# Making the first four tiles' queries in two halves, in a fused decoder layer on one core

## The reference, cut to what matters

```python
x = _layernorm(x + _L0_attn_ref(x, ...))      # S4D long convolution by FFT, then its own layernorm
x = _layernorm(x + _L0_xattn_ref(x, ctx, ctx, ...))   # 16 heads of 16 over 77 keys
x = _layernorm(x + _L0_ffn_ref(x, ...))       # gated MLP of 1024 plus product-key experts
# cross attention:
qh = (q @ Wq.T + bq).reshape(B, Nq, H, D).transpose(0, 2, 1, 3)
attn = jax.nn.softmax(jnp.einsum('bhqd,bhkd->bhqk', qh, kh) * scale, axis=-1)
return (attn @ vh).transpose(0, 2, 1, 3).reshape(B, Nq, C) @ Wo.T + bo
```

## Time and profile before

| | |
|---|---|
| median of three runs | 693.98 us (689.98 to 695.78) |
| the profiled execution's own time | 689.71 us |
| its span | 687.9 us |
| TensorE matmul busy | 599.0 us (87%), 3200 instructions |
| VectorE, ScalarE, GpSimd busy | 484.3, 403.9, 308.5 us |
| mean granted TensorE clock | 0.920 of full speed |

### The profile page before, as it was taken

One profiled execution on the slowest core, in us unless ns is written; L12 is line 12 of the kernel. 1 busy time (PEld: TensorE's weight loads), 2 busy tenths in 40 slices (PEclk: granted clock), 3 DMA queues, 4 the chain that ended last, 5 costly groups with the idle time before them and its releaser, 6 DMA issues.

```text
span 687.9 us, 9791 instructions
## 1 busy us (share of the span) xinstructions
PE 599.0 (87%) x3200; PEld 393.4 (57%) x3200; DVE 484.3 (70%) x955; ACT 403.9 (59%) x595; POOL 308.5 (45%) x354
## 2 busy tenths in 40 slices
PE   6809588795769598999999999999999999899896
PEld 2503477573636364454776745578565478453485
DVE  7976475662346885897857789765779796678782
ACT  3865446222143265996673878773778774677760
POOL 3704975554142456352263632243735243744441
PEclk9858879899695677999999999999999999999999
DMA  8994020368161000000000000000000000000000
GB/s 272 309 235 90 1 76 27 101 171 224 27 247 59 1 1 1 0 2 0 1 0 1 17 8 9 0 1 1 8 16 1 9 1 1 9 15 9 0 9 23
DMA packets 19613, 34.14 MB, mean 50 GB/s; under 512 B 7273, under 2 KB 13931, under 8 KB 18219
## 3 DMA queue, kind: packets, MB, share of 16 engines
q1 hardware_dynamic: 15179, 29.33, 14.8%
q10 hardware_dynamic: 4384, 4.20, 1.9%
HBM read 21.81 MB, written 10.65 MB: 47 GB/s over the span
## 4 chain that ended last, share of the span: by engine, by line
PE 64%; DVE 12%; DMA 6%; ACT 6%; POOL 6%; issue 5%; SPq 1%; DVEq 0%; POOLq 0%; ACTq 0%
PE banks L804 20%; PE banks L894 8%; PE banks L899 8%; PE banks L849 4%; PE banks L871 4%; PE banks L826 3%; DMA scr_x<-arena 3%; PE banks L861 3%; PE banks L679 2%; PE banks L746 2%; PE banks L835 2%; DMA scr_v<-arena 2%; PE banks L886 2%; DVE stats L1437 2%; PE banks L716 1%
## 5 line engine op out<-in xcount | busy, mean ns | idle before, releaser
L1260 POOL TENSOR_TENSOR arena<-arena 128x1024 f32<-128x1024 f32 x64 | 123.3, 1927 | 159.1 <-ACT arena L1122 158.3
L804 PE MATMUL banks<-arena 128*128 128x512 f32 x384 | 174.4, 596 | 5.3 <-issue 3.7
L804 PEld LDWEIGHTS banks<-arena 128*128 128x128 f32 x384 | 69.8, 190 | 83.0 <-issue 76.9
L1122 ACT ACTIVATE arena<-arena 128x1024 f32<-128x1024 f32 x64 | 73.5, 1149 | 7.5 <-DVE arena L1525 3.0
L1124 ACT ACTIVATE arena<-arena 128x1024 f32<-128x1024 f32 x64 | 73.5, 1149 | 2.1
L1525 DVE SCALAR_TENSOR_TENSOR arena<-arena 128x1024 f32<-128x1024 f32 x48 | 63.9, 1331 | 1.7
L1012 ACT COPY arena<-banks 128x512 f32<-128x512 f32 (+1 forms) x64 | 34.1, 532 | 46.2 <-PE banks L796 30.3
L894 PE MATMUL banks<-arena 128*128 128x256 f32 x256 | 58.4, 381 | 2.4 <-DVE arena L1547 2.2
L1233 POOL TENSOR_SCALAR arena<-mv 128x1 f32<-128x1 f32 (+1 forms) x40 | 14.4, 361 | 102.1 <-DVE mv L1438 100.7
L899 PE MATMUL banks<-arena 128*128 128x256 f32 x256 | 57.9, 379 | 0.0
L1026 ACT ACTIVATE tok<-tok,arena,rstd 128x256 f32<-128x256 f32 x48 | 27.9, 598 | 44.0 <-POOL arena L1238 43.0
(11 more groups left out here) (179 smaller groups left out, 1096.3 us busy)
## 6 DMA issues: line engine op xcount, KB each, us to landing
scr_x<-arena SPq DMA_DIRECT2D x16, 256.0 KB, 8.9
arena<-scr_x SPq DMA_DIRECT2D x4, 1024.0 KB, 11.0
scr_z<-arena ACTq DMA_DIRECT2D x14, 256.0 KB, 3.8
tok<-in_x SPq DMA_DIRECT2D x8, 256.0 KB, 6.1
arena<-scr_z SPq DMA_DIRECT2D x4, 512.0 KB
out<-tok SPq DMA_DIRECT2D x16, 128.0 KB, 1.7
arena<-scr_z SPq DMA_DIRECT2D x2, 640.0 KB
arena<-in_imat SPq DMA_DIRECT2D x1, 1152.0 KB, 5.5
```

The source lines that it names most:

```text
L804: ins = mm(bk[:, :], w[:, k, P * m:P * m + P], src[:, k, :], start=(k == 0), stop=(k == KC - 1))
L1122: fn(ebuf[m % 2], sxb[m % 2], ACT.Prelu, bias=negt[:, n % 2, h:h + 1], alpha=FAR).then_inc(s_ranked, 1)
L1260: tt(sxb[m % 2], sim[:, n % 2, h, 0:XR].unsqueeze(2).broadcast_to((P, XR, NKEYS)), sim[:, n % 2, FH + h, :].unsqueeze(1).broadcast_to((P, ...
```

## The change

The queries of group 0 are made in two halves of 256 tokens (two tiles) each. Half 0 needs only turn1(0,0), half 1 needs turn1(0,1). Each half is a matmul of 256 columns instead of 512, twice as often, and takes a PSUM bank of its own; ScalarE moves each half by itself. Scores of tiles 0 and 1 wait for half 0, those of tiles 2 and 3 for half 1. The other three groups are made as before.

```diff
+         "query_first": (-0.08, -0.07, 0.114, 0.2684), "score_first": (0.0, 0.108), "turn2": (-0.001, 0.0655),
-         "ln": (-1.672, -1.4036, 0.3158, 1.2242, 1.9402, 2.3725, 3.0344, 3.1428),
-         "ln_steps": (-0.409, -0.234, 0.162, 0.013, 0.361), "sines": (-2.943, -2.336), "tables": (0.152,),
+         "ln": (-1.721, -1.4035, 0.316, 1.2245, 2.021, 2.373, 3.035, 3.1435),
+         "ln_steps": (-0.347, -0.234, 0.162, 0.013, 0.361), "sines": (-2.943, -2.336), "tables": (0.152,),
...
-       ("dve", "ln"): -0.302, ("dve", "residual"): -0.025, ("pool", "turn1"): 0.518, ("pool", "turn2"): 0.089,
+       ("dve", "ln"): -0.518, ("dve", "residual"): -0.025, ("pool", "turn1"): 0.518, ("pool", "turn2"): 0.089,
...
     def queries(start, s):
         for kind in ("turn1", "query"):
             for j in range(2):
-                put(start, kind, s, j, j=j)
+                if kind == "query" and s == 0:
+                    for half in range(2):
+                        put(start, kind, s, j, half, key="query_first", j=2 * half + j)
+                else:
+                    put(start, kind, s, j, j=j)
...
     for h in range(2):
-        put(-1, "score", 0, h, j=h)
+        put(-1, "score", 0, h, key="score_first", j=h)
...
+        def query_of(tl, hh):
+            return ("query", 0, hh, tl // 2) if tl < SUPER else ("query", tl // SUPER, hh)
+        def query_cols(step):
+            return slice(W // 2 * step[3], W // 2 * (step[3] + 1)) if step[1] == 0 else slice(0, W)
...
-                    pe.wait_ge(s_tev, T_AT[("turn1", n, 1)] + 1)
-                    wide(step + ("a",), wq, step[2], x1T)
+                    pe.wait_ge(s_tev, T_AT[("turn1", n, step[3] if n == 0 else 1)] + 1)
+                    wide(step + ("a",), wq, step[2], x1T, query_cols(step))
...
-                    pe.wait_ge(s_wact, ACT_TURN[("query", n // SUPER, hh, "a")])
+                    pe.wait_ge(s_wact, ACT_TURN[query_of(n, hh) + ("a",)])
...
-                    fn(qT[:, j, :], src, ACT.Identity, bias=pcol[:, j:j + 1]).then_inc(s_wact, 1)
+                    fn(qT[:, j, query_cols(step)], src[:, query_cols(step)], ACT.Identity,
+                       bias=pcol[:, j:j + 1]).then_inc(s_wact, 1)
```

More of the change, by code:

```diff
@@ L55 @@
 PAIRS = [(0, NC)] + [(2 * m - 1, 2 * m) for m in range(1, FREQ - 1)] + [(NC - 1,)]
[L58 to L63, removed]
-         "ln": (-1.672, -1.4036, 0.3158, 1.2242, 1.9402, 2.3725, 3.0344, 3.1428),
-         "ln_steps": (-0.409, -0.234, 0.162, 0.013, 0.361), "sines": (-2.943, -2.336), "tables": (0.152,),
+PLACE = {"probs": (0.166, 0.2592, 0.441), "score": (0.273, 0.6341), "attend": (0.592,), "turno": (0.772,),
+         "project": (1.4,), "project_last": (0.934,), "turn1": (-0.087, 0.0432), "query": (0.245, 0.2685),
+         "query_first": (-0.08, -0.07, 0.114, 0.2684), "score_first": (0.0, 0.108), "turn2": (-0.001, 0.0655),
+         "sim": (0.379,), "sim_first": (0.031,), "best": (0.432,), "best_first": (0.207,),
+         "pair": (0.283, 0.3903, 0.7922, 0.8026), "total": (0.847,), "first": (-0.1,), "sums": (-0.805,),
+         "exps": (-0.131,), "late": (-0.027, 0.0082, 0.7012),
+         "conv": (-2.338, -1.7115, -1.497, -1.4195, -1.329, -1.2905, -1.172, -0.9595),
+         "ln": (-1.721, -1.4035, 0.316, 1.2245, 2.021, 2.373, 3.035, 3.1435),
+         "ln_steps": (-0.347, -0.234, 0.162, 0.013, 0.361), "sines": (-2.943, -2.336), "tables": (0.152,),
          "taps": (0.982,), "x_second": (-2.2, 0.237), "skip": (1.3, 0.3), "k_first": (5.915, 0.66, 9.6, 0.247),
@@ L69 @@
          "inverse": (9.103, 0.13, 10.25, 0.11), "products": (0.0, 1.0, 0.0, 0.996, 0.0, 0.802, -0.084, 0.975),
-         "probs_alone": (0.016, 0.079, 0.473), "score_alone": (0.367, 0.6874), "attend_alone": (0.566,),
+         "probs_alone": (0.016, 0.0791, 0.4732), "score_alone": (0.367, 0.6875), "attend_alone": (0.566,),
          "turno_alone": (0.734,), "project_alone": (0.979,), "dev2": (0.031,), "norm2": (0.093,), "dev3": (0.402,),
@@ L798, in turn_tokens, with wide @@
                 ins.then_inc(s_tmm, 1)
-            def wide(key, w, m, src):
+            def wide(key, w, m, src, cols_of=slice(0, W)):
                 bk = w_unit(key)
                 for k in range(KC):
-                    ins = mm(bk[:, :], w[:, k, P * m:P * m + P], src[:, k, :], start=(k == 0), stop=(k == KC - 1))
+                    ins = mm(bk[:, cols_of], w[:, k, P * m:P * m + P], src[:, k, cols_of], start=(k == 0), stop=(k == KC - 1))
                 ins.then_inc(s_wmm, 1)
@@ L1051, in _ @@
                     if n:
-                        act.wait_ge(*W_DONE[W_AT[("query", n - 1, KC - 1, "a")]])
+                        act.wait_ge(*W_DONE[W_AT[query_of(SUPER * n - 1, KC - 1) + ("a",)]])
                     turned_tokens(step, step[2], x1T)
```

## The result

The changed kernel takes 686.76 us (median of 11 runs, 684.66 to 689.97) against 692.68 us for the kernel before in 11 runs beside it. The ratio is 0.9923 (95% interval 0.9895 to 0.9950): 5.3 us faster, between 3.5 and 7.3. The forecast was 691.0 us and a gain of 3.0 us, with a range of 686.5 to 695.5. The time lies in the range, 0.26 us above its low end, and inside the 1% that I called no change. Of the 4.2 us between forecast and time, 1.3 come from the kernel before, whose median was 693.98 us in the three runs that the forecast starts from and 692.68 in the eleven here. The mechanism and its sign were right; one term was too small.

What follows compares the result with a forecast made beforehand. The ramp's serial first tiles, with no engine full, bounded what could change. 3.6 us won at the probabilities' transposes less 0.65 given back makes 2.95, say 3.0: 691.0 us against a median of 693.98, range 686.5 to 695.5.

Steps and rivals of the forecast that it cites:

- (a): GpSimd at the start: dev1 0 goes before dev0 1, takes 1.59 us instead of 2.24 and ends at 190.58.
- (b): ScalarE at the start: norm1 0 runs from 190.62 to 191.72 instead of from 191.32.
- (c): TensorE: half queries of 0.93 us end at 194.5 and 195.4, half reads take 0.48, score(0,0) runs to 196.25.
- (e): VectorE: score(0,0) from 196.3 to 197.95 and score(0,1) from 199.5 to 201.15, no ln between them.
- (f): ScalarE: exponentials wait behind second-half queries; probabilities' transposes start at 203.05 instead of 206.69, 3.6 us earlier.
- (d): Price of GpSimd's swap: residual 1 starts at 191.7 instead of 188.86; norm1 1 ends 2.75 us later.
- What is given back: At turno 1 on TensorE: ln 5 before attend 1 on VectorE makes it wait, losing 0.65 us of the gain.
- What is kept behind it: From tile 0's transposes to the end: 3.6 us carried to project 0, 2.95 to 3.0 to turn2(0,0) and the end.
- rival 2: Tile 0 and turno 2 to project 2: full clock holds, 3 us more gain, 688.0 us; chance 0.20.
- The carrying: From turno 1 on: 2.95 to 3.0 us of gain reaches turn2(0,0) and the end of the kernel.
- Rival 1: Ramp: clock falls before 198 us and is half from 249 to 257; 2.3 us slower, 696.3 us; chance 0.12.
- rival 3: Behind the start: an unseen wait takes the gain, nothing carried, 694 us; chance 0.18.

Runs made afterwards that it cites:

- e2: Changed kernel with the old numbers for ln, ln_steps and VectorE's ln offset, so halves without the new lists: ratio 0.9941 to the kernel before.
- e1: Kernel before with the new numbers for ln, ln_steps and VectorE's ln offset, queries whole: ratio 1.0073 to the kernel before, 5 us slower.
- e3: Changed kernel with ln 5 back behind attend 1 on VectorE: ratio 0.9934 to the kernel before.
- e4: Changed kernel with dev1 4 back ahead of dev2 1 on GpSimd: ratio 0.9958 to the kernel before, 2.9 us faster.
- e9: Kernel before with four half queries put where the two whole ones stood, old numbers for everything else: ratio 0.9959 to the kernel before.
- e10: Kernel before with ln 2 to ln 5 moved into VectorE's idle time, queries whole: ratio 0.9976 to the kernel before.
- e8: Changed kernel with 18 idle products on TensorE in its pause before conv 0: ratio 0.9932 to the kernel before.
- e11: Changed kernel with ln 2 to ln 5 moved into VectorE's waits: ratio 0.9835 to the kernel before; medians of all executions 684.17 against 691.17 us.
- e6: Kernel before with idle products filling TensorE's pauses in the ramp: ratio 0.9962 to the kernel before, 2.6 us faster.
- e7: Changed kernel with idle products filling TensorE's pauses in the ramp: ratio 0.9900 to the kernel before, from four executions.
- e12: Kernel of e11 with 24 idle products before conv 0 and more in the ramp: ratio 0.9820 to the kernel before; medians 680.71 against 690.65 us.

## Why the prediction was right

**The start.** 3.26 us at the transposes against 3.6. The times of steps (a), (b), (c) and (e), counted from residual 0, stand within 0.3 us. Residual 1 starts at 6.38 us (forecast 6.3) and norm1 1 at 11.63 (11.4). Step (f) named what decides: the exponential behind query(0,1,1). Its two half queries took 1.99 us and not 1.85.

**The price of GpSimd's swap, step (d).** It is there (2.94 us at residual 1) but costs nothing at the transposes: without it they come at 18.17 (e2). The sentence that the first half alone would have allowed more left out conv 7. With whole queries the same swap, with the rest of the new lists, costs 5 us (e1).

**What is given back.** 0.65 us at turno 1: 0.70 in the trace (5.36 less 4.66), 0.76 in e3. **What I cost at nothing**, dev2 1 before dev1 4: nothing (e4).

**The step that was too small.** "What is kept behind it" carried 3.6 us to project 0 and let TensorE keep the half clock of before, 8.0 us from the transposes on. It took 4.3 us (206.02 to 210.36), because the clock held; project 0 moved by 5.36 us. I had that as one half of rival 2, with 1.4 to 2 us and a chance of 0.20, and wrote that nothing in the rows fixes when the clock falls. The other half of rival 2, full clock at turno 2 and project 2, did not come: turno 2 took 0.69 us and project 2 1.97, both at half. And the reason that I gave for the first half was wrong: the clock did not fall at 207 us, the old time of day, but at 211.3, behind attend 0. It was not chance either: the clock had fallen by tile 0's transposes in both traces of before and in e1, e9 and e10, and held to the end of attend 0 in all six traces with score(0,0) moved forward and no idle products at tile 0 (after, e2, e3, e4, e8, e11). What I should have looked at is TensorE's pauses ahead of that step: 1.90 and 2.95 us with one score product of 0.79 us between them before (both traces), and 1.76 us now. With the pauses filled the clock stays full past project 1 in both kernels (e6, e7), so it is for want of work in the pauses that it falls. Their length alone does not fix when: with 1.90 and 2.60 us (e10) it fell and came back before attend 0, and in the changed kernel the products behind a pause of only 1.52 us, after attend 0, ran at half clock. So the rows of before name the place, but not whether the clock would hold there.

This term, 2.1 us, makes most of the difference: with it the gain is 4.66 us at project 1, where the forecast had 2.95. The timed 5.3 us (3.5 to 7.3) fits that and can't be told from 4.7. The Trainium skill, TensorE: Matmul & The Clock Gate, "HAM oscillation — how this bites in real kernels", which I had used for a rival against the change, has short bursts with longer waits between them start each next burst at half rate. These traces agree in direction, for the change took pauses away and the clock held longer; the page's waits are longer than the 1.90 and 2.95 us here.

**The carrying.** 4.66 us at project 1, 4.72 at turno 2, 4.5 to 4.9 at turn2(0,0) (e4 and e8 against the two traces of before). The 7.3 us at the end of the first trace are not all the change's: 1.8 of them are the sim product at full clock. Rival 1 (slower clock) and rival 3 (nothing carried) fall.

**The signs.** Of those that I named as right, dev1 0 (5.18 us from residual 0, named 5.2), norm2 1 (233.17, named before 234) and the first steps came; "3.0 us between every step behind it" did not, it was 4.7. One sign of being wrong was met in the first trace: turn2(0,0) is 5.48 us earlier, over the 5 that I had set. In e4 and e8 it is 4.5 to 4.9. On the span's own scale it stands at 259.27, near the 259.2 that I named, but that is luck: the ramp started 2.6 us later in that execution. The range of 9 us holds even the time before (693.98), so that a median within it says little by itself; the steps say more.

## What to carry to other kernels

When a serial chain starts a kernel's steady part, cut the first product so that the first unit can leave before the second arrives, and then look for what stands in the same queue behind the unit that is late: here that was conv 7 and the second half's reads. Look at the pauses that an edit removes from TensorE as well as the time on the path, for at project 0 the clock was worth 2.2 us beside 3.1 for the steps. And fill another engine's waits with work that is due later anyway: moving four statistics brought as much as the split in the one trace of e10, though the timed runs show only 1.6 us of it (-0.4 to 3.7), and it was free on top of the split (e11).

## What the runs showed of the hardware that I had not expected

- The half clock was kept through dense work: from 206.7 to 219.4 us in the kernel before TensorE was busy 12.2 of 12.7 us at 0.50. In e10, with the transposes only 0.34 us earlier, it was half for the transposes and back at full for attend 0 (2.32 us). What decides between these two I did not settle.
- In e8 and e12 the clock fell only after work had begun again: 0.8 us into conv 0 behind a pause of 4.32 us, and 0.1 us into it behind one of 3.79 us. In the changed kernel the products behind a pause of 1.76 us ran at full clock, and those behind one of 1.52 us, later in the same trace, at half. The length of the last pause alone does not decide.
- Four GpSimd instructions on 128x2 took 2.24 us beside VectorE's two-input work and 1.61 us without it.
